# Second input batch and all results by row-indexed transfers from GpSimd in a two-batch attention and mixture kernel

## The reference

```
sa, ca, ga, sb, cb, gb = six rows of silu(c[b]) @ wmod          # the modulation; ga, gb kept at least 0.25 in size
h = layernorm(x) * (1 + ca) + sa
x = x + ga * (h + attention(h) @ Wo.T + bo + 0.1 * quantum(h))   # causal, pruned by a distance threshold
h = layernorm(x) * (1 + cb) + sb
x = x + gb * mixture(h)                                          # 16 routed experts, top 4, and 2 shared ones, F = 128
```

## Time and profile before

| | us |
|---|---|
| median of 2 runs | 731.34 (731.22 to 731.46) |
| span of the profiled execution | 734.6 |
| inputs and attention of batch 0 | 0 to about 230 |
| mixture of batch 0 with inputs and attention of batch 1 | about 230 to 559 |
| mixture of batch 1 | about 559 to 734.6 |
| PE busy in the span | 598.6 (81%) |
| DVE busy | 591.6 (81%) |
| POOL busy | 380.8 (52%) |
| ACT busy | 373.8 (51%) |

### The profile page before, as it was taken

One profiled execution on the slowest core, in us unless ns is written; L12 is line 12 of the kernel. 1 busy time (PEld: TensorE's weight loads), 2 busy tenths in 40 slices (PEclk: granted clock), 3 DMA queues, 4 the chain that ended last, 5 costly groups with the idle time before them and its releaser, 6 DMA issues. The chain is left out here.

```text
span 734.6 us, 11508 instructions
## 1 busy us (share of the span) xinstructions
PE 598.6 (81%) x3660; PEld 336.8 (46%) x3660; DVE 591.6 (81%) x1573; ACT 373.8 (51%) x729; POOL 380.8 (52%) x333
## 2 busy tenths in 40 slices
PE   2675859695957798898989899789788678989895
PEld 1544436463652243343545455355454345555553
DVE  3768799998797999757976887767986988888876
ACT  0222547375733344556785688646345344545443
POOL 8349453827602424569876566714124345555553
PEclk9996679897978999999998999989999999999998
DMA  7101001100000000000000000000000000000000
GB/s 197 51 1 33 1 1 33 33 1 2 1 0 1 0 1 2 12 3 1 0 1 15 1 1 1 0 16 1 1 2 14 1 1 16 2 15 2 16 1 15
DMA packets 14052, 9.13 MB, mean 12 GB/s; under 512 B 1557, under 2 KB 12841, under 8 KB 13993
## 3 DMA queue, kind: packets, MB, share of 16 engines
q1 hardware_dynamic: 13992, 8.41, 4.0%
HBM read 6.31 MB, written 2.10 MB: 11 GB/s over the span
## 5 line engine op out<-in xcount | busy, mean ns | idle before, releaser
L538 POOL TENSOR_TENSOR gp<-stage,gp 128x512 f16<-128x512 f32 x144 | 167.4, 1162 | 241.0 <-ACT gp L677 222.7
L677 ACT CAST gp<-stage 128x512 f16<-128x512 f32 x144 | 88.3, 613 | 85.6 <-DVE stage L1474 84.3
L664 ACT ACTIVATE stage<-bank 128x512 f32<-128x512 f32 x144 | 84.8, 589 | 36.0 <-PE bank L722 35.7
L630 ACT COPY ptr<-bank 128x512 f32<-128x512 f32 (+2 forms) x80 | 41.5, 519 | 80.9 <-PE bank L854 80.0
L869 PE MATMUL bank<-v,ptr 128*128 128x128 f32 x544 | 79.1, 288 | 2.0 <-DVE x L1241 2.0
L869 PEld LDWEIGHTS bank<-v,ptr 128*128 128x128 f32 x544 | 72.9, 204 | 4.2 <-ACT ptr L630 1.6
L1474 DVE SCALAR_TENSOR_TENSOR stage<-bank,stage 128x512 f32<-128x512 f32 x72 | 49.7, 690 | 24.8 <-ACT stage L664 24.3
L720 PE MATMUL bank<-wd,gp 128*128 128x128 f16 x288 | 52.4, 221 | 20.5 <-POOL gp L538 17.1
L503 POOL TENSOR_TENSOR row<-row,dx 128x512 f32<-128x512 f32 (+3 forms) x48 | 54.5, 1141 | 25.3 <-ACT dx L575 25.3
L1456 DVE SCALAR_TENSOR_TENSOR ysb<-bank,comb,ysb 128x128 f32<-128x128 f32 x240 | 67.0, 342 | 0.0
L720 PE MATMUL bank<-h,wg 128*128 128x512 f16 x144 | 55.8, 387 | 13.2 <-DVE hid L1398 13.1
(11 more groups left out here) (267 smaller groups left out, 1412.5 us busy)
## 6 DMA issues: line engine op xcount, KB each, us to landing
out_x<-x SPq DMA_DIRECT2D x8, 256.0 KB, 2.3
stage<-in_L_ffn_gate_w SPq DMA_DIRECT2D x1, 576.0 KB, 7.5
stage<-in_L_ffn_up_w SPq DMA_DIRECT2D x1, 576.0 KB, 4.3
stage<-in_L_ffn_down_w SPq DMA_DIRECT2D x1, 576.0 KB, 4.2
stage<-in_L_ffn_gate_w SPq DMA_DIRECT2D x1, 448.0 KB, 7.0
stage<-in_L_ffn_up_w SPq DMA_DIRECT2D x1, 448.0 KB, 3.5
stage<-in_L_ffn_down_w SPq DMA_DIRECT2D x1, 448.0 KB, 3.5
row<-in_L_wmod SPq DMA_DIRECT2D x1, 384.0 KB
```

The lines of the kernel that those rows point to most:

```text
L538: pool.tensor_tensor(gp[:, s % 3, 1, :], act_g[:, s % 2, :], gp[:, s % 3, 0, :], ALU.subtract)\
L664: act.activation(sg[:, s % 2, :], gate_bank(s)[:, :], func, scale=half_of / (H_UP * W_UP))\
L677: act.copy(gp[:, (s - 1) % 3, 0, :], act_g[:, (s - 1) % 2, :]).then_inc(act_high, 1)
```

## The change

SP no longer loads `x` of batch 1 and no longer stores anything. POOL does both, with `indirect_dma_start`: each transfer moves 128 rows of 512 bytes, one to or from each partition, and the row of each partition is read from a new tile `token` (128 partitions x 32 indices, value 128*block + partition), which one more `iota` fills at the start. The rows so addressed are the same as before.

`fetch` of the 16 blocks of batch 1 stands in `inputs(0, 22)`, ahead of the fifth part of `base(0, 0, ...)`, which is called further down in the same function. `store(f)` waits for `out_ready` number `f+1` and issues four transfers, one a block. It is called at the end of POOL's `step(s)`: after steps 22, 40, 58 and 76 for batch 0, after steps 91, 109 and 127 for three chunks of batch 1, and at s = 145, when POOL has no more work, for the last. In all there are 16 + 32 = 48 transfers issued by POOL in place of 9 issued by SP. SP's last wait is for all 32 stores.

```diff
--- before.py
+++ after.py
@@ -192,6 +192,7 @@
         minus_half = sb("minus_half", [P, BLK]); half = sb("half", [P, 1])
         w_up = sb("w_up", [P, 1])
         warm = sb("warm", [P, 1])
+        token = sb("token", [P, NB * BLK], U32)
         qp = sb("qp", [P, BLK, 2]); qc = sb("qc", [P, BLK, 2]); sq = sb("sq", [P, BLK, 2])
         nrm = sb("nrm", [P, BLK]); unit = sb("unit", [P, BLK, 2])
         part = sb("part", [P, 2]); mean = sb("mean", [P, 2])
@@ -230,6 +231,7 @@
 
 
         small_loaded = sem("small_loaded"); x_loaded = sem("x_loaded")
+        x_fetched = sem("x_fetched")
         consts_ready = sem("consts_ready"); pool_step = sem("pool_step")
         set_pe = sem("set_pe")
         set_act = sem("set_act")
@@ -367,8 +369,6 @@
             for dst, src in ((btq_bc, btq), (rb_bc, router_b)):
                 sp.dma_start(dst[:, :], src.rearrange("(o d) -> o d", o=1).broadcast_to([P, dst.shape[1]]))\
                   .then_inc(small_loaded, 16)
-            sp.wait_ge(x_loaded, 16)
-            sp.dma_start(x[:, BLK:, :], batch_view(hs)[:, BLK:NB * BLK, :]).then_inc(x_loaded, 16)
             for n in range(6):
                 routed, shared = ((gate_w.rearrange("e d f -> d e f"), sh_gate_w.rearrange("d (s f) -> d s f", s=NS)),
                                   (up_w.rearrange("e d f -> d e f"), sh_up_w.rearrange("d (s f) -> d s f", s=NS)),
@@ -383,13 +383,7 @@
                 else:
                     sp.dma_start(dst[:, 0:E - PIECE, :], routed[:, PIECE:E, :]).then_inc(stage_loaded[1], 16)
                     sp.dma_start(dst[:, E - PIECE:PIECE, :], shared).then_inc(stage_loaded[1], 16)
-            with sp.Fori(0, NB * CH) as it:
-
-                sp.wait_ge(out_ready, it + 1)
-                sp.dma_start(batch_view(out)[:, bass.ds(it * PER, PER), :],
-                             x[:, bass.ds(it * PER, PER), :]).then_inc(stored, 16)
-
-            sp.wait_ge(stored, 16 * NB * CH)
+            sp.wait_ge(stored, 16 * NB * BLK)
 
         @block.gpsimd
         def _(pool):
@@ -410,6 +404,7 @@
             chain.step(pool.memset(minus[:, :], 0.0))
             chain.step(pool.memset(identb[:, :], 0.0))
             chain.step(pool.iota(iotai[:, :], pattern=[[1, E]], base=0, channel_multiplier=0))
+            chain.step(pool.iota(token[:, :], pattern=[[P, NB * BLK]], base=0, channel_multiplier=1))
             w_den = float(N) * N - 1
             for n, wgt in enumerate((4.0, 8.0, 4.0, -2.0, 2.0 * N)):
                 chain.step(pool.memset(vw[:, n:n + 1], wgt / w_den))
@@ -439,6 +434,21 @@
             chain.step(pool.memset(fl[:, :, 21:24], HUGE))
             chain.settle()
             pool.sem_inc(consts_ready, 1)
+
+            hs_rows = hs.rearrange("b n d -> (b n) d")
+            out_rows = out.rearrange("b n d -> (b n) d")
+
+            def fetch(i):
+
+                pool.indirect_dma_start(x[:, i, :], None, hs_rows,
+                                        bass.IndirectOffsetOnAxis(token[:, i:i + 1], 0)).then_inc(x_fetched, 16)
+
+            def store(f):
+
+                pool.wait_ge(out_ready, f + 1)
+                for i in range(f * PER, (f + 1) * PER):
+                    pool.indirect_dma_start(out_rows, bass.IndirectOffsetOnAxis(token[:, i:i + 1], 0),
+                                            x[:, i, :], None).then_inc(stored, 16)
 
             def power(dst, src, exponent, count):
 
@@ -505,6 +515,9 @@
             def inputs(b, k):
                 if k == STATS + CH - 1:
                     power(rs[:, :], ve[:, :], minus_half[:, :], ROOTS * b + 1)
+                if b == 0 and k == BASE + 4:
+                    for i in range(BLK, NB * BLK):
+                        fetch(i)
                 if b == 0 and k in (NORM, POSITIONS + 5):
                     split(0 if k == NORM else 1)
                 if k == POSITIONS:
@@ -537,6 +550,10 @@
                         pool.wait_ge(down_made, s - 2)
                     pool.tensor_tensor(gp[:, s % 3, 1, :], act_g[:, s % 2, :], gp[:, s % 3, 0, :], ALU.subtract)\
                         .then_inc(act_split, 1)
+                if ends_chunk(s, 5) and smooth(s - 5):
+                    store((s - 5) // EX)
+                if ends_chunk(s, 2) and not smooth(s - 2):
+                    store((s - 2) // EX)
 
             def late(b, t):
                 pass
@@ -1010,7 +1027,10 @@
             def input_stats(b, g):
 
                 if g == 0:
-                    dve.wait_ge(x_loaded, 16 * (b + 1))
+                    if b:
+                        dve.wait_ge(x_fetched, 16 * BLK)
+                    else:
+                        dve.wait_ge(x_loaded, 16)
                 blocks = range(g * PER, (g + 1) * PER)
                 for i in blocks:
                     step(dve.bn_stats(st[:, i, :], x[:, b * BLK + i, :]))
```

## The result

The changed kernel takes 771.92 us (771.32 to 772.52, 2 runs) against 731.34 us (731.22 to 731.46): 5.5% slower, ratio 1.0546 with a 95% interval of 1.0496 to 1.0596. That is 40.6 us more, inside the range given, and nearly twice the 22.1 us of the forecast's sum.

A forecast was written before the change was run, and what follows sets the result against it. The prediction saw the kernel bound by a slackless loop through POOL, PE, DVE and ACT, not by POOL's throughput. Its terms, 0.1 + 1.6 + 2.5 + 3.0 + 0.1 + 0 + 10.4 + 4.4 = 22.1 us, gave 753.4 us, range 740 to 778.

The forecast's parts named there:

- The price t = 1.2 us: Time one row-indexed transfer of 128 rows occupies POOL: taken as 1.2 us, bounded by 0.56 and 2.9 us.
- POOL locked out by DVE: Rival: DVE's work holds up POOL's transfers, making each around 2 us; 57 us in all, 788 us; chance 0.15 including other causes.
- Cheap transfer: Rival: a transfer costs POOL only 0.56 to 0.95 us and idle time covers most; around 739 us, chance 0.24.
- Start: Program start: the added `iota` costs about 0.1 us; removing SP's load of batch 1's `x` gains nothing.
- The fetch, 1.6 us: Batch 0's first `base`: 16 transfers delay the first norm's root queued behind them on POOL, by 1.6 us.
- Stores 0 to 3: After steps 22, 40, 58 and 76: losses of 2.5, 3.0, 0.1 and 0 us beyond idle time and DVE's cover.
- the sign given at the prediction's end: Check in the changed profile: steps 77 to 80 must be unmoved against step 76.
- Stores 4 to 6, 10.4 us: After steps 91, 109 and 127, batch 1's mixture: each store delays the slackless loop by 3.46 us, 10.4 in all.
- 4t - 1.34: Delay per store after steps 91, 109 and 127: four transfers less 1.34 us hidden by the wait for `out_ready`; 3.46 us.
- the 4.22 us of the loop: Batch 1's mixture: two steps take 4.22 us between `gp` starts, expected unchanged between the stores.
- Store 7, 4.4 us: Program end: four transfers made one after the other, the last landing after that, cost 4.4 us.
- The base of the sum: The profiled execution of before, span 734.6 us, was put 3.3 us above the runs' median of 731.34 us.

The follow-up runs named there:

- e6: Kernel before, but POOL stores each chunk by one 256 KB block transfer, SP still loading batch 1's `x`: 733.17 us, ratio 0.9995.
- e10: Kernel before, but POOL loads batch 1's `x` as one 1 MB block and stores each chunk as one 256 KB block: 731.87 us, ratio 0.9995.
- e4: Kernel before, but POOL fetches batch 1's `x` in 16 row-indexed transfers, placed early behind its first split; SP stores: 738.76 us, ratio 1.0106.
- e3: Kernel before, with SP's load of batch 1's `x` moved behind the first two pieces of expert weights: 731.30 us, ratio 0.9986.
- e9: Kernel before, but POOL fetches batch 1's `x` in four lots of four row-indexed transfers at its idle places; SP stores: 730.88 us, ratio 0.9968.
- e11: Kernel before with only the stores by POOL's row-indexed transfers, plus 18 unused PE matmuls in each of three pauses: 757.14 us, ratio 1.0342.
- e7: Kernel before with POOL storing seven chunks by row-indexed transfers; SP loads batch 1's `x` and stores the last chunk: 757.91 us, ratio 1.0313.
- e8: Kernel before, SP storing, with POOL doing four unused subtractions after steps 91, 109 and 127 and no transfers: 748.30 us, ratio 1.0195.

## Why the prediction was right, and where its sum was not

*The price t = 1.2 us.* Right: 1.26. It was the step on which the forecast said it hung, and it did put the time on the right side. That it came out so near is in good part luck. It was picked between 0.56 and 2.9 us by likeness to a root of 128 x 4 numbers, with the work of two addresses a row as the reason. Rows are not what POOL's time goes by in the block form: 512 rows took 0.78 us and 2048 rows 1.39 (e6, e10). With t = 1.26 the forecast's own sum is 24.8 us, so the price accounts for under 3 of the 18.5 us that the sum is short.

The Trainium skill (Perfetto Trace Analysis, DMA Instruction — SWDGE (GPSIMD)) says that the profile's duration of such an instruction ends with the writing of descriptors and not with the moving of the data. The trace agrees: the first store after step 91 has its instruction from 628.06 to 629.04 us, and its data moved from 629.6 to 629.9.

*POOL locked out by DVE.* Not seen: 48 transfers took 0.94 to 1.24 us whatever DVE did. In e4 some ran beside the very `xn` instructions of which the prediction spoke, and took 0.94 to 1.20.

*Cheap transfer.* Wrong for this form, right for the block form (0.78 us for 512 rows, e6), which gave no loss. The rule of the Trainium skill that making descriptors is small (DMA: Bandwidth & Descriptors, Anatomy of one DMA) holds by these rows for a block transfer; here four row-indexed ones took over 6 times as long as one block of the same data. The prediction has a slip in this rival: its sum passes 14.6 us at t = 0.96 and not at 0.98. The lock-out's sum at t = 2 has one too: its terms add up to 59 us and not 57.

*Start.* Forecast 0.1 lost and no gain. The new `iota` took 0.15 us. The trace shows 1.3 us gained at the root of the positions and nothing that reaches the time (e3).

*The fetch, 1.6 us.* This is the first term that was mis-sized, and its mechanism was not the one at work: 9.3 us measured. The forecast asked who is queued behind 16 transfers on POOL, and there the cover was what it said (6.35 us of idle were left ahead of the root, and the first `base` ended at 87.4, ahead of the 87.99 at which DVE had needed it). It took for granted that the other engines run on undisturbed. Beside a long train DVE and ACT see PE's results up to 8 us late (e4), beside four transfers they don't (e9). With the same 16 transfers in lots of four nothing is lost, and with one block of 1 MB at the same place neither (e10), so the cause is shown as far as that; why a long train does this is open.

*Stores 0 to 3.* Forecast 2.5 + 3.0 + 0.1 + 0 = 5.6 us. Read step by step the changed kernel shows 3.5 + 3.2 + 0.6 + 0 = 7.3, and the whole stage 3.5 to 7.7, depending on whose clock dips it is held against. So this part was sized nearly right, 1 us short at the first store. After the fourth, `gp` of step 77 is late by 2.1 us and on time again by step 80. That agrees with the term, but not with the sign given at the prediction's end, that steps 77 to 80 must be unmoved.

*Stores 4 to 6, 10.4 us.* This is the second term that was mis-sized: 17.3 us. Its own mechanism is exact, 4t - 1.34 = 3.70 at t = 1.26 and 3.73 to 3.75 in the timelines, 11.2 us in e11. What was missing is the clock: after each of these pauses of 5.4 us PE came back at half clock, which adds 5.6 to 6.1 us for the three. The forecast even read the 4.22 us of the loop as fixed "in between".

*Store 7, 4.4 us.* 6.3 us. From `x` being ready to SP's last branch it took 6.4 us in place of 2.6, 3.8 more, a little less than the forecast's 4.4. The other 2.5 are a term that the forecast put at nothing: it let the end be when the data lands, and POOL's own drain outlasts SP by 2.7 us. With SP as the issuer of the last chunk no time is lost at the end (e7), because the drain then runs beside SP's transfer.

*The base of the sum.* The profiled execution of before was put at 3.3 us above the median by its span. By what the later runs show of spans and times it was 5 us above, and much of that in the steps 22 to 91. That is no error in the price of the change, but it is why one pair of traces gave 36 us where the runs gave 40.6.

So the side and the range were right, and by the right mechanism for about half of the loss: the sum at the measured t is 24.8 us, of which the fetch's 2.6 did not come about as forecast. Of the 18.5 us missing from the forecast's 22.1, some 7.7 are the fetch's, 6.9 lie in stores 4 to 6, most of them the clock's, 1.9 at the end, and up to 2 in the smooth steps. That the time still fell inside the range is partly luck too: the range was made wide for an unknown t, and 771.92 us is what the sum gives for t = 1.6, which is not the t that was measured.

## What to carry to other kernels

A delay on an engine that feeds TensorE is not paid once: look for how long TensorE will stand still, and if it is several us, add what its matmuls cost at half clock right after. Where a side engine has to issue many small transfers, count instructions and not bytes, take a block transfer if the rows allow it, and otherwise give each idle gap one transfer, or four, not sixteen. Let another engine issue the last store of a program, so that the drain of the engine that issued the others runs beside it.

## What was not expected of the hardware

- Beside a train of 16 row-indexed transfers by POOL (1.25 us each), waits of DVE and ACT for PE ended 1.1 to 8.1 us late, none before the ninth transfer, and up to 3 us after the last one; waits for DVE did not, and beside trains of four none did. In e4 PE had started its next matmuls on time, so it had not stopped there; whether the ends of its matmuls or only their signals were late can't be told from these traces, since PE's ends are modelled. Whether the number of transfers in a row or the time of 10 us counts is open too; trains of five to fifteen were not run.
- TensorE's granted clock fell to 1.2 GHz for 3.4 to 6.8 us at every pause of about 5 us (4.8 us in e8, 5.4 in the changed kernel) in a stretch that was at 2.4 GHz throughout before, and 18 matmuls without use in the pause kept it at 2.4 and made the stage 5.6 us shorter than without them.
- One row-indexed transfer of 128 rows holds POOL for 1.26 us, one block transfer of 512 rows for 0.78 and of 2048 rows for 1.39.
- POOL's drain at the end of the program grew by 0.08 us for every row-indexed transfer that POOL had made, however long ago: it ended 0.07 us after POOL's last work with none, 1.40 with 16, 2.38 with 28, 2.69 with 32, 3.68 with 44 and 3.99 with 48. In the changed kernel that was 2.7 us after SP had seen all of them land.
- Executions of kernels with the same work in a stage differ by up to 4 us in batch 0's stages, by where the clock dips, and by 0.1 us in batch 1's mixture.
